# Attention scores of a transformer block on one core: six two-bank units per batch against four three-bank groups

## The chip, the core and the metric

The kernel runs on one core of a Trainium2 chip. The core's engines work in parallel, each on its own list of instructions in order, and wait for each other by semaphores: TensorE (PE in the profile, its weight loads PEld), VectorE (DVE), ScalarE (ACT), GpSimd (POOL) and SyncE (SP), which here issues the DMA transfers. The metric is the device time of one execution in microseconds (us). Matmul results go to PSUM, 8 banks of 512 float32 per partition.

## The reference

For 16 batches of 256 tokens with 256 features: a layer norm, then `x + attention(xn) + ffn(xn)`.

```
x + _L0_attn_ref(xn, w_qkv, w_out) + _L0_ffn_ref(xn, w_gating, w_linear)
attention, 16 heads of 16:  scores = where(causal, q k^T / 4, -1e10)
                            out = softmax(scores) v ;  out @ w_out
ffn, operands rounded to fp8: (gelu(x wg0) * (x wg1)) @ w_linear
```

## The kernel before

It has two phases. **The first** (lines 290 to 457 and 690 to 728) normalises the tokens in 8 chunks of 512, transposes them, and runs the feed-forward layer; the transposed tokens, split into a high and a low part (`xt_part`), are stored for the second phase (`xt_store`). The queries, keys and values of batch 0 and the queries and keys of batch 1 are already made inside it (`first_batches`).

**The second phase** is attention, one batch after another, software-pipelined by hand: the loops over `s` at the end of each engine's program name, stage by stage, which piece of which batch comes next. Nothing but this written order and the semaphores sets the sequence. A batch passes through these pieces:

- `project_qk` (L738) and `project_v` (L745): 12 matmuls each of 256 columns over all 128 rows of the array, into one of the two banks of `misc` (banks 6 and 7). `project_qk` is called twice a batch, for u = 0 and 1, eight heads each. ACT copies the result to `qk_raw` (`copy_qk`, L592), DVE rounds it to the high part (`round_qk`, L476), POOL subtracts for the low part (`split_qk`, L339), and SP issues three transfers that lay the parts out in `stack` (`fill_stack`, L228).
- The scores are computed twice. First for the row maxima (`max_scores`, L781): queries against keys, with the causal mask added by bf16 matmuls of a selection matrix (`pick`) and a triangle (`above`) (L773). DVE reduces each bank to the maxima (`find_max`, L494). `transpose_max` (L827) turns them, ACT negates them (`negate_max`, L606), and SP places them as one more row of `stack` (`place_max`, L233). Then again, transposed and with the maximum already subtracted by that row (`exp_scores`, L799); ACT takes the exponential into `arena` (`exponent`, L613) and POOL zeroes the part above the diagonal (`mask`, L352).
- `times_v` (L818): probabilities times values, 32 matmuls on four column tiles of the array, for c = 0 and 1. DVE transposes (`o_to_rows`, L501) and divides by the row sums (`normalize_o`, L507 to L516); ACT and POOL split the result (L622, L357), `project_out` (L835, 6 matmuls for each c) multiplies by the output weights, ACT copies (`copy_y`, L628), POOL adds the residual (L362), and SP stores.

All score matmuls use 63 or 64 rows of the array; those for u = 0 lie on the lower half of the rows and those for u = 1 on the upper, so that two run side by side. A batch has six **units** (`UNITS`), three for each half c of the heads: one unit of four heads with 128 keys, two of two heads with 256. A unit fills two banks. The maxima rotate over three banks (`max_ps`, banks 0 to 2), the exponentials have one pair (`exp_ps`, banks 3 and 4), and `times_v` has bank 5 (`pv_ps`). Unit n of batch s for the maxima and unit n of batch s-1 for the exponentials stand next to each other in the order; between such blocks stand the projections, the transposes and `times_v`. Stage `s` begins on PE with `exp_scores(s - 1, 0)`.

## Time and profile before

| | us |
|---|---|
| median of 3 runs | 386.46 |
| lowest and highest | 383.99, 386.74 |
| the profiled execution | 387.27 |
| its span in the trace | 385.5 |
| busy: PE, DVE, ACT, POOL | 357.1, 281.6, 222.9, 198.2 |

In the rows below a line starts with the time in us at which a group of instructions starts and the time it takes, then the engine, the source line, the operation, the tiles written and read, and the shape. Consecutive instructions of one line are merged ("x12"). Matmuls overlap in the records: what a block costs on PE is read from its start to the start of the next block, not from its duration.

### The profile page before, as it was taken

The numbers are of one execution on the slowest core, as the hardware profiler recorded it, in microseconds if no ns is written. First come the engines' busy times: TensorE is split into PE (matmuls) and PEld (weight loads), VectorE is DVE, ScalarE is ACT, GpSimd is POOL, SyncE is SP. The second block draws the span as 40 slices with busy tenths as digits, with TensorE's granted clock in tenths as the row PEclk, the third lists the DMA queues.
The fourth block names the chain that finished last, engine by engine and source line by source line (L and its number), as shares of the span: only waits on it lengthen the run. The fifth ranks groups of instructions, "written<-read, shape, count | busy, mean of one in ns | idle before, by whom it ended". The sixth has DMA issues, their size and how long they took to land.

```text
span 385.5 us, 9835 instructions
## 1 busy us (share of the span) xinstructions
PE 357.1 (93%) x3882; PEld 269.8 (70%) x3882; DVE 281.6 (73%) x540; ACT 222.9 (58%) x352; POOL 198.2 (51%) x236
## 2 busy tenths in 40 slices
PE   6698999998989799999999999999999999998884
PEld 6354455447474678788888888888888888885563
DVE  5778788876626657988778778878787887788832
ACT  0885666764645165656665656656666566574751
POOL 2352530333231234654847748568467485685575
PEclk9999999999999989999999999999999999998988
DMA  7986734940638114506347255274372562542002
GB/s 240 321 283 193 210 110 120 237 147 0 234 95 274 55 67 157 195 29 221 96 155 247 77 175 187 72 239 136 115 247 84 169 193 79 172 137 68 21 30 82
DMA packets 45453, 57.52 MB, mean 149 GB/s; under 512 B 2656, under 2 KB 36960, under 8 KB 45408
## 3 DMA queue, kind: packets, MB, share of 16 engines
q1 hardware_dynamic: 45408, 56.90, 45.8%
q8 instruction: 31, 0.51, 0.5%
q14 instruction: 14, 0.11, 0.1%
HBM read 16.78 MB, written 12.58 MB: 76 GB/s over the span
## 4 chain that ended last, share of the span: by engine, by line
PE 80%; DVE 8%; ACT 6%; issue 3%; DMA 1%; POOL 1%; POOLq 0%; DVEq 0%; SPq 0%; ACTq 0%
PE ps L738 12%; PE ps L818 12%; PE ps L799 11%; PE ps L781 8%; PE ps L726 7%; PE ps L745 7%; PE ps L835 6%; PE ps L773 4%; PE ps L706 4%; PE ps L699 4%; DVE act L457 4%; PE ps L827 2%; PE ps L675 2%; ACT arena L613 2%; ACT gate L562 2%
## 5 line engine op out<-in xcount | busy, mean ns | idle before, releaser
L494 DVE TENSOR_REDUCE row_max<-ps 128x2 f32<-128x512 f32 (+1 forms) x192 | 123.6, 686 | 43.9 <-PE ps L781 43.3
L613 ACT ACTIVATE arena<-ps 128x1024 f32<-128x1024 f32 x96 | 98.5, 1026 | 75.0 <-PE ps L799 75.0
L352 POOL TENSOR_SCALAR_AFFINE_SELECT arena<-arena 128x512 f32<-128x512 f32 (+1 forms) x96 | 73.7, 787 | 72.4 <-ACT arena L613 72.2
L799 PE MATMUL ps<-stack 64*128 64x256 f32 (+1 forms) x512 | 52.6, 305 | 4.1 <-ACT arena L613 4.1
L738 PE MATMUL ps<-xs,wq_part 128*128 128x256 f32 x384 | 53.7, 289 | 2.1 <-DVE wq_part L448 0.7
L457 DVE TENSOR_TENSOR act<-ps,gate 128x512 fp8e4<-128x512 f32 x64 | 43.1, 686 | 13.7 <-ACT gate L562 12.0
L781 PE MATMUL ps<-stack 63*128 63x256 f32 (+1 forms) x512 | 51.9, 301 | 0.0
L818 PE MATMUL ps<-arena,v_aug 128*32 128x256 f32 (+1 forms) x1024 | 50.6, 340 | 0.9 <-DVE xn L501 0.9
L738 PEld LDWEIGHTS ps<-xs,wq_part 128*128 128x128 f32 x384 | 48.7, 192 | 3.5 <-DVE wq_part L448 1.0
L799 PEld LDWEIGHTS ps<-stack 64*128 64x128 f32 x512 | 36.8, 190 | 18.1 <-issue 7.3
L562 ACT ACTIVATE gate<-ps 128x512 bf16<-128x512 f32 x64 | 38.0, 598 | 17.3 <-PE ps L699 11.1
L339 POOL TENSOR_TENSOR qk_part<-w_raw,qk_part 128x512 fp32r<-128x512 f32 x32 | 40.8, 1276 | 6.8 <-DVE qk_part L476 6.8
L706 PE MATMUL ps<-x,wg 128*128 128x512 fp8e4 x128 | 38.0, 378 | 4.9 <-DVE act L457 4.5
L818 PEld LDWEIGHTS ps<-arena,v_aug 128*32 128x32 f32 x1024 | 29.8, 113 | 17.3 <-issue 1.8
L699 PE MATMUL ps<-x,wg 128*128 128x512 fp8e4 x128 | 38.0, 379 | 2.1 <-ACT gate L562 1.0
L357 POOL TENSOR_TENSOR xt_part<-xn,xt_part 128x256 fp32r<-128x256 f32 x32 | 26.9, 841 | 23.8 <-ACT xt_part L622 23.7
L781 PEld LDWEIGHTS ps<-stack 63*128 63x128 f32 x512 | 36.4, 189 | 0.3
L773 PE MATMUL ps<-above,pick 64*128 64x128 bf16 (+1 forms) x384 | 31.0, 240 | 2.7 <-DVE row_max L494 2.7
L290 POOL TENSOR_SCALAR var_eps<-mean_var 128x4 f32<-128x4 f32 x8 | 2.1, 264 | 59.7 <-DVE mean_var L406 59.7
L835 PE MATMUL ps<-wq_part,xt_part 128*128 128x256 f32 x192 | 30.7, 296 | 0.8 <-ACT w_raw L628 0.7
L501 DVE STREAM_TRANSPOSE xn<-ps 128x512 f32<-128x512 f32 x32 | 22.8, 712 | 10.9 <-PE ps L818 10.9
L726 PE MATMUL ps<-wl,act 128*128 128x256 fp8e4 x256 | 29.4, 272 | 0.3 <-issue 0.3
(57 smaller groups left out, 440.7 us busy)
## 6 DMA issues: line engine op xcount, KB each, us to landing
stack<-qk_part SPq DMA_DIRECT2D x96, 256.0 KB, 3.0
xt_store<-xt_part SPq DMA_DIRECT2D x16, 512.0 KB, 4.1
xs<-xt_store SPq DMA_DIRECT2D x16, 512.0 KB, 4.3
out_dram<-w_raw SPq DMA_DIRECT2D x16, 256.0 KB, 4.3
xres<-in_L_attn_x_dram SPq DMA_DIRECT2D x7, 512.0 KB, 7.1
arena<-in_L_ffn_w_gating_dram SPq DMA_DIRECT2D x2, 1024.0 KB, 9.9
stack<-spare SPq DMA_DIRECT2D x4, 512.0 KB, 7.2
arena<-in_L_ffn_w_linear_dram SPq DMA_DIRECT2D x1, 1024.0 KB, 14.0
```

What stands on the lines that cost most here:

```text
L352: nc.gpsimd.affine_select(diag, diag, pattern=[[0, 1024 // width], [1, P]], compare_op=ALU.is_ge, fill=0.0, base=0, channel_multiplier=-1) ...
L457: nc.vector.tensor_tensor(act8[:, j, :], up_ps[j % 2][:], gate[:, j % 2, :], ALU.mult, saturate=False).then_inc(act_done, 1)
L494: nc.vector.tensor_reduce(row_max[:, b % 2, qt, col:col + heads], max_ps[:, place, :].rearrange("p (h k) -> p h k", k=width), axis=AXIS_X, ...
L613: nc.scalar.activation(arena[:, n, :, :], exp_ps, ACT.Exp).then_inc(exp_done, 1)
L699: last = nc.tensor.matmul(gate_ps[j % 2][:], wg8[:, 0, k, j * P:(j + 1) * P], x8[:, k, :], start=(k == 0), stop=(k == KD - 1))
L706: last = nc.tensor.matmul(up_ps[j % 2][:], wg8[:, 1, k, j * P:(j + 1) * P], x8[:, k, :], start=(k == 0), stop=(k == KD - 1))
L726: last = nc.tensor.matmul(down_ps[i][:, t * D:(t + 1) * D], act8[:, j, tok:tok + P], wl8[:, j, :], start=(j == 0), stop=(j == J - 1))
L738: last = nc.tensor.matmul(misc[:, 1, s * S:(s + 1) * S], wq_part[:, a, kt, col:col + P], xs[b % 2][:, z, kt, :], start=(i == 0), stop=(i = ...
L781: last = nc.tensor.matmul(max_ps[:, (2 * unit + u) % 3, i * width:(i + 1) * width], st[rows, j0 + i, 0, qt * P:(qt + 1) * P], st[rows, j0 ...
L799: last = nc.tensor.matmul(exp_ps[:, u, i * width:(i + 1) * width], st[rows, j0 + i, 1, kt * P:(kt + 1) * P], st[rows, j0 + i, 0, kt * P:S] ...
L818: last = nc.tensor.matmul(pv_ps[32 * i:32 * i + 32, u * S + kt * P:(u + 1) * S], va[:, kt, 2 * (HG * c + i) + u, :], cols, start=(kt == 0) ...
L835: last = nc.tensor.matmul(misc[:, 0, t * D:(t + 1) * D], ot_part[:, z, c, t * P:(t + 1) * P], wq_part[:, a, c, 3 * D:4 * D], start=(c == t ...
```

## The change

The scores of a batch come in four **groups** of three banks. Group (c, ii) fills the two first banks with one unit's two halves u, as before: for ii = 0 the four heads with 128 keys, for ii = 1 two heads with 256. Its third bank takes two heads with 256 keys of one half u = ii alone. The exponentials get banks 0 to 2 and the maxima banks 3 to 5; `times_v` moves to the two banks of `misc`, which it now shares with the projections, so that these are placed and waited for in another way (`pv_bank`, and the waits written out in the loop of PE).

On PE one function `scores(maxima, exps)` writes a block: all six mask matmuls of the group, the maxima of two banks, the exponentials of two banks (of another group), and then the third banks of both in turn, one matmul on one half of the rows and one on the other. The whole group waits, ahead of its masks, until DVE has reduced all three banks of the group before. DVE reduces two banks with one instruction of 1024 elements and the third with one of 512; ACT and POOL likewise have one instruction for two banks and one for the third. The rounding of queries and keys (`round_qk`) goes from DVE to ACT, which now reads the PSUM bank twice in `copy_qk`. `project_qk` writes one bank for u = 0 and the other for u = 1, both calls stand side by side in a stage, and so do `project_v` and both calls of `project_out`. The stages of all engines are written anew.

The banks, and the function that writes a block on PE:

```
-        max_ps, exp_ps, pv_ps, misc = ps[:, 0:3, :], ps[:, 3:5, :], ps[:, 5, :], ps[:, 6:8, :]
+        exp_ps, max_ps, misc = ps[:, 0:3, :], ps[:, 3:6, :], ps[:, 6:8, :]
...
+            def scores(maxima, exps):
+
+                if maxima:
+                    b, c, ii = maxima
+                    g = GROUPS * b + 2 * c + ii
+                    st = stack[b % NB]
+                    if g >= 1:
+                        pe.wait_ge(max_done, 2 * g)
+                    heads, width = (2, 2 * P) if ii else (4, P)
+                    for i in range(2):
+                        for u in range(2):
+                            put_mask(u, slice(64 * u, 64 * u + 64), heads, i)
+                        put_mask(2, slice(64 * ii, 64 * ii + 64), 2, i)
+                    if ii == 0:
+                        pe.wait_ge(stacked[c], 48 * (b + 1))
...
+                    if ei == 0:
+                        pe.wait_ge(neg_in[ec], 16 * (eb + 1))
+                    if h >= 1:
+                        pe.wait_ge(exp_done, 2 * h - 1)
...
+                if exps and h >= 1:
+                    pe.wait_ge(exp_done, 2 * h)
...
+                        last_max = nc.tensor.matmul(max_ps[:, 2, cols], st[rows, 4 * c + i, 0, P:S], st[rows, 4 * c + i, 1, :],
+                                                    start=False, stop=(i == 1), skip_group_check=True)
...
+                        last_exp = nc.tensor.matmul(exp_ps[:, 2, cols], est[rows, 4 * ec + i, 1, 0:P], est[rows, 4 * ec + i, 0, :],
+                                                    start=True, stop=True)
```

The copies of queries and keys on ACT:

```
             def copy_qk(b, g):
                 act.wait_ge(qk_ready[g], b + 1)
                 if b >= 1:
+                    act.wait_ge(stacked[g], 48 * b)
+                made = misc[:, g, :].rearrange("p (a s) -> p a s", a=2)
+                nc.scalar.copy(qk_part[:, g, QHI:KLO, :], made).then_inc(qk_hi[g], 1)
+                if b >= 1:
                     act.wait_ge(qk_lo[g], b)
-                nc.scalar.copy(qk_raw[:, g, :, :], misc[:, 1, :].rearrange("p (a s) -> p a s", a=2)).then_inc(qk_copied[g], 1)
+                nc.scalar.copy(qk_raw[:, g, :, :], made).then_inc(qk_copied[g], 1)
```

The new loop on PE, its calls and two of its waits:

```
+            for s in range(B + 3):
+                if has(s) or has(s - 2):
+                    scores((s, 0, 0) if has(s) else None, (s - 2, 1, 1) if has(s - 2) else None)
...
+                    project_qk(s + 1, 0)
...
+                    project_qk(s + 1, 1)
...
+                if has(s) or has(s - 1):
+                    scores((s, 0, 1) if has(s) else None, (s - 1, 0, 0) if has(s - 1) else None)
+                if has(s - 1) and s < B:
+
+                    pe.wait_ge(*((qk_copied[1], s + 2) if has(s + 1) else (o_by_q_done, turned(s - 2, 0))))
+                    transpose_max(s - 1, 1)
...
+                    times_v(s - 2, 1)
+                if has(s) or has(s - 1):
+                    scores((s, 1, 0) if has(s) else None, (s - 1, 0, 1) if has(s - 1) else None)
...
+                    project_v(s + 1)
...
+                    for c in range(2):
+                        project_out(s - 3, c)
...
+                if has(s) or has(s - 1):
+                    scores((s, 1, 1) if has(s) else None, (s - 1, 1, 0) if has(s - 1) else None)
...
+                    transpose_max(s, 0)
...
+                    times_v(s - 1, 0)
```

The loop on SP:

```
-            for s in range(B + 5):
-                if s >= 2 and has(s):
-                    fill_stack(s, 1)
-                if has(s - 1):
+            for s in range(B + 3):
+                if s == B:
                     place_max(s - 1, 1)
                 if s >= 1 and has(s + 1):
                     fill_stack(s + 1, 0)
+                    fill_stack(s + 1, 1)
+                if has(s - 1) and s < B:
+                    place_max(s - 1, 1)
```

On PE in a middle stage, before, from the masks of unit 0 to the exponentials of unit 1 (L773 masks, L781 maxima, L827 transposes of the maxima, L738 queries and keys, L799 exponentials):

```order
L773 MATMUL ps<-above,pick 128x4x64 [waits max_done]
L773 MATMUL ps<-above,pick 128x4x64 x3
L781 MATMUL ps<-stack 128x128 [waits stacked0]
L781 MATMUL ps<-stack 128x128 x7
L827 MATMUL ps<-ident,row_max 8x128 [waits max_done,v_done]
L827 MATMUL ps<-ident,row_max 8x128
L738 MATMUL ps<-xs,wq_part 128x256 [waits qk_copied0]
L738 MATMUL ps<-xs,wq_part 128x256 x11
L773 MATMUL ps<-above,pick 128x2x64 [waits max_done]
L773 MATMUL ps<-above,pick 128x2x64 x3
L781 MATMUL ps<-stack 128x256 x4
L799 MATMUL ps<-stack 128x256 [waits exp_done]
```

The same engine in the changed kernel, the first block of a stage (L771 masks, L793 maxima of two banks, L810 exponentials of two banks, L821 and L825 the third banks):

```order
L771 MATMUL ps<-above,pick 128x4x64 [waits max_done]
L771 MATMUL ps<-above,pick 128x4x64
L771 MATMUL ps<-above,pick 128x2x64
L771 MATMUL ps<-above,pick 128x4x64 x2
L771 MATMUL ps<-above,pick 128x2x64
L793 MATMUL ps<-stack 128x128 [waits stacked0]
L793 MATMUL ps<-stack 128x128 x7
L810 MATMUL ps<-stack 128x256 [waits exp_done]
L810 MATMUL ps<-stack 128x256 x3
L821 MATMUL ps<-stack 128x256 [waits exp_done]
L825 MATMUL ps<-stack 128x256
```

The masks of three banks stand ahead of the maxima, and the matmuls of one and a half units of each kind now stand in one block, between which and the next stand 24 matmuls over all rows or the transposes with `times_v`.

On SP, the transfers of one middle stage before (L233 negated maxima, L228 queries and keys, L218 tokens, L238 result):

```order
L228 DMA stack<-qk_part 32x4x512 [waits exp_ready,qk_lo1]
L228 DMA stack<-qk_part 32x8x256 x2
L233 DMA stack<-neg_max 2x4x256 [waits neg_done1]
L228 DMA stack<-qk_part 32x4x512 [waits exp_ready,qk_lo0]
L228 DMA stack<-qk_part 32x8x256 x2
L218 DMA xs<-xt_store 128x1024 [waits v_ready]
L238 DMA out_dram<-w_raw 128x2x256 [waits y_done]
L233 DMA stack<-neg_max 2x4x256 [waits neg_done0]
```

and in the changed kernel (L245 negated maxima, L240 queries and keys):

```order
L240 DMA stack<-qk_part 32x4x512 [waits exp_ready,qk_lo0]
L240 DMA stack<-qk_part 32x8x256 x2
L240 DMA stack<-qk_part 32x4x512 [waits exp_ready,qk_lo1]
L240 DMA stack<-qk_part 32x8x256 x2
L245 DMA stack<-neg_max 2x4x256 [waits neg_done1]
L230 DMA xs<-xt_store 128x1024 [waits v_ready]
L250 DMA out_dram<-w_raw 128x2x256 [waits y_done]
L245 DMA stack<-neg_max 2x4x256 [waits neg_done0]
```

The negated maxima of c = 1 now stand behind all six transfers of a batch's queries and keys.

## Rows read from the trace of the kernel before

**Rows 1.** The page: busy time of each engine, its share of the span, instructions.

```profile
PE 357.1 (93%) x3882; PEld 269.8 (70%) x3882; DVE 281.6 (73%) x540; ACT 222.9 (58%) x352; POOL 198.2 (51%) x236
```

**Rows 2.** Stretches (us): length, busy time of each engine, granted clock, DMA share, GB/s.

```profile
126.00:165.00 39.00, 35.64 (x439) 29.18 (x436) 28.26 (x48) 20.03 (x28) 16.11 (x18) 0.96 0.37 124
165.00:341.00 176.00, 176.00 (x2344) 147.23 (x2342) 140.23 (x254) 107.13 (x160) 113.33 (x124) 1.00 0.45 146
341.00:385.50 44.50, 34.33 (x440) 25.07 (x432) 26.14 (x48) 22.34 (x33) 28.20 (x33) 0.90 0.22 73
```

**Rows 3.** Timeline of PE, the first half of a middle stage.

```profile
226.45 0.66 PE L799 MATMUL ps<-stack 64*128 64x128 f32 x8
226.95 0.39 PE L773 MATMUL ps<-above,pick 64*128 64x256 bf16 x4
227.10 0.64 PE L781 MATMUL ps<-stack 63*128 63x128 f32 x8
227.67 0.38 PE L827 MATMUL ps<-ident,row_max 128*8 128x128 f32 x2
227.81 1.68 PE L738 MATMUL ps<-xs,wq_part 128*128 128x256 f32 x12
229.42 0.29 PE L773 MATMUL ps<-above,pick 64*128 64x128 bf16 x4
229.52 0.48 PE L781 MATMUL ps<-stack 63*128 63x256 f32 x4
229.84 0.40 PE L799 MATMUL ps<-stack 64*128 64x256 f32 x4
230.17 1.68 PE L745 MATMUL ps<-wq_part,xs 128*128 128x256 f32 x12
231.78 0.51 PE L799 MATMUL ps<-stack 64*128 64x256 f32 x4
...
232.63 1.51 PE L818 MATMUL ps<-arena,v_aug 128*32 128x256 f32 x32
234.06 0.66 PE L799 MATMUL ps<-stack 64*128 64x128 f32 x8
```

**Rows 4.** Timeline of PE: two adjoining blocks over all rows, and the next stage's start.

```profile
237.17 0.98 PE L835 MATMUL ps<-wq_part,xt_part 128*128 128x256 f32 x6
...
239.51 0.50 PE L799 MATMUL ps<-stack 64*128 64x256 f32 x4
...
241.81 0.66 PE L799 MATMUL ps<-stack 64*128 64x128 f32 x8
```

**Rows 5.** Timeline of PE: the first masks, and the starts of stages 3 and 15.

```profile
126.40 0.39 PE L773 MATMUL ps<-above,pick 64*128 64x256 bf16 x4
165.05 0.66 PE L799 MATMUL ps<-stack 64*128 64x128 f32 x8
347.81 0.55 PE L799 MATMUL ps<-stack 64*128 64x128 f32 x6
```

**Rows 6.** Timelines of DVE (two reductions) and of ACT (a copy, an exponential), middle stage.

```profile
230.04 1.29 DVE L494 TENSOR_REDUCE row_max<-ps 128x2 f32<-128x512 f32 x2 [0.97 <-PE ps L781]
226.09 0.61 ACT L592 COPY w_raw<-ps 128x512 f32<-128x512 f32 x1
227.15 1.02 ACT L613 ACTIVATE arena<-ps 128x1024 f32<-128x1024 f32 x1 [0.46 <-PE ps L799]
```

**Rows 7.** A stretch of the end, columns as in the second group.

```profile
352.80:356.00 3.20, 3.20 (x40) 0.53 0.00 0
```

**Rows 8.** The page: the subtraction for the low parts, mean ns and idle before.

```profile
L339 POOL TENSOR_TENSOR qk_part<-w_raw,qk_part 128x512 fp32r<-128x512 f32 x32 | 40.8, 1276 | 6.8 <-DVE qk_part L476 6.8
```

**Rows 9.** Waits from 341 us on: us in total, times, longest.

```profile
ACT arena L613 <- PE ps L799: 11.6, 12, 3.0
```

**Rows 10.** One line at a time: issue times in ns (min/median/max) and landing (us).

```profile
L228 SPq DMA_DIRECT2D stack<-qk_part x96: 542/606/1675, 97.8 to 346.4; - x96
DMA to landing us min/median/max: 2.4/3.0/5.7
```

More of the change, by code:

```diff
@@ L516, in normalize_o @@
                 nc.vector.transpose(ot_raw[:, c, :], o_norm[:, :]).then_inc(ot_ready, 1)
-            for s in range(B + 3):
-                if has(s - 1):
-                    find_max(s - 1, 5)
-                if s >= 1 and has(s + 1):
-                    round_qk(s + 1, 0)
+            for s in range(B + 2):
                 if has(s - 2):
@@ L752, in first_batches, with put_mask @@
                 pe.wait_ge(ffn_done, 2 * (CHUNKS - 2 + b))
-                project_qk(b, 0)
+                for g in range(2):
+                    project_qk(b, g)
                 if b == 0:
+                    pe.wait_ge(qk_copied[0], 1)
                     project_v(0)
-                pe.wait_ge(qk_copied[0], b + 1)
-                project_qk(b, 1)
             ffn_steps(step, first_batches)
-            def max_scores(b, n):
-                unit = UNITS * b + n
-                st = stack[b % NB]
-                heads, qt = (4, 0) if n % 3 == 0 else (2, 1)
+            def put_mask(bank, rows, heads, i):
@@ L784, in max_scores @@
[L784 to L802 removed]
+                first = width - P + 64 * i
@@ L840, in _ @@
             pe.wait_ge(act_done, J * CHUNKS)
+            pe.wait_ge(xt_lo, KD * CHUNKS)
             pe.wait_ge(spare_made, 1)
[L842 to L894 removed]
```

304 lines of the change are left out of this document (136 added, 168 removed).

## The prediction

> **What bounds the kernel.** I read the busy shares first: PE is busy 93% of the span, DVE 73% [rows 1]. A share says little by itself, so I cut the span into stretches [rows 2]. From 165 to 341 us PE is busy for 176.00 of 176.00 us at full granted clock; the list of waits for that stretch has none of PE's. DVE works 140 of the 176 us, ACT 107, POOL 113. So 45% of the run is a steady loop in which only PE's own time counts, and the rest is a first phase, the filling of the pipeline (35.6 of 39 us busy) and its emptying (34.3 of 44.5 us).
>
> In the loop the timeline of PE repeats every 241.81 - 226.45 = 15.36 us, one stage for one batch [rows 3, 4]. What counts is start to start. Two things are to be seen. Twelve matmuls over all rows take 1.61 us (L745, 230.17 to 231.78), but 18 in a row, from the second half of `project_out` to the end of `project_qk`, take 2.34 (237.17 to 239.51). So one more costs 0.12 us, and twelve of these are 1.48: about 0.15 us are paid for entering and leaving the block. Score blocks pay too: four masks, four maxima and four exponentials take 0.75 us where the masks come first (229.42) and 0.85 where the exponentials do (231.78). A stage has six score blocks, so six returns to the full array.
>
> **The change on PE in a steady stage.** The number of matmuls and their columns per batch are the same: masks 8 x 256 + 16 x 128 = 4096 columns before, and 2 x (4 x 256 + 2 x 128) + 2 x (6 x 128) = 4096 after. Removed are the switches. Block by block, from starts in [rows 3]:
>
> - A group with ii = 0: masks about 0.35 us (four 256-column masks take 0.15, 226.95 to 227.10, where both halves of the rows work side by side; the third bank's masks lie on one half and hold it up, 0.1 each); eight maxima 0.57 less the switch of 0.09, 0.48; four exponentials 0.24 (229.84 to 230.17 less 0.09); four matmuls of the third banks, on alternate halves, also 0.24; the switch 0.09. Sum 1.40.
> - A group with ii = 1: masks 0.22 (0.10 and 0.06 for each mask of the third bank), four maxima 0.32 (229.52 to 229.84), eight exponentials 0.44 (0.50 less the entry), third banks 0.24, switch 0.09. Sum 1.31.
> - 24 matmuls over all rows, twice: 1.61 + 12 x 0.12 = 3.05 each.
> - Transposes with `times_v` behind them, twice: 0.14 + 1.44 = 1.58 each.
>
> 2 x (1.40 + 1.31 + 3.05 + 1.58) = 14.68 us, against 15.36. For the masks the bounds are 0.1 us less a group (they overlap after all) and 0.1 more.
>
> The transposes used to be followed by full-array matmuls, now by `times_v` on 32-column tiles. No row shows that pair; the nearest are transposes into `project_qk`, contained in the 0.14, and scores into `times_v`, in the 0.09. The bounds are 0 and 0.15 a time; I take 0, as the transposes already pay on leaving the scores. The Trainium skill (TensorEngine Tiling (Array Packing), Key Properties) says that changing the tiling mode drains the engine. The 0.09 to 0.15 us at every change between blocks agree with it; by that rule the step from transposes to `times_v` is one more change of mode, and it would speak against this part of the edit.
>
> **What the others must deliver by then.** I lay one stage out from its first mask at 0. DVE starts 0.52 us after a block of four maxima starts (229.52, 230.04), that is 0.2 after the next block's start [rows 3, 6]; behind a switch, which holds the next block up by 0.1, I count 0.1.
>
> - DVE. Two reductions of 512 take 1.29 us, one 0.69 [rows 6], so one of 1024 is 1.2 to 1.3. In a ii = 1 group maxima are ready at 0.22 + 0.52 = 0.74; DVE is done with two banks at 2.0 and with the third at 2.65. The next group's masks come 1.31 + 1.58 = 2.89 after. That wait is covered by 0.2 us, the thinnest margin on DVE; behind ii = 0 the spacing is 4.45 and the margin large. DVE loses the two roundings and is busy some 12 of 14.7 us.
> - ACT. The second copies add 2 x 0.5 us; with exponentials 4 x (1.03 + 0.58) = 6.4 and the rest it is busy 11.4 of 14.7 us. The wait before the first transposes is for the second copy of u = 1: ready at 1.40 + 3.05 + 0.1 = 4.55, two copies of 0.6 overlapping by 0.1 [rows 6] end at 5.65, and the transposes stand at 4.45 + 1.31 = 5.76. Covered, by 0.1.
> - SP. The low parts are subtracted by POOL in 1.28 us [rows 8]: for u = 0 they are ready at 5.5, for u = 1 at 6.95. Six issues of 0.61 us with what lies between them [rows 10] run from 5.55 to 9.4; only then goes the transfer of the negated maxima of c = 1, which were ready at 7.4. The last group of the stage, at 1.40 + 3.05 + 1.31 + 1.58 + 1.40 + 3.05 = 11.8, needs them for its exponentials, 0.54 later at 12.3. The trace does not give its landing; the transfers ahead of it land after 2.4 us at best, 3.0 in the median, 5.7 at worst [rows 10]. That is 11.8, 12.4 or 15.1. I take 12.4, the median, since the six before it are just such transfers: a wait of 0.1. The Trainium skill (DMA: Bandwidth & Descriptors, Anatomy of one DMA) has a fixed cost of about 2.0 us for a transfer on GpSimd's path; if SP's were alike it would land at 11.4, and the wait would be nought.
>
> Period 14.68 + 0.1 = 14.8 us. PE goes through twelve stages between the third and the fifteenth: before 347.81 - 165.05 = 182.8 us (the last of them lacks half of its projection) [rows 5], after 12 x 14.8 = 177.6. **Gain 5.2 us.**
>
> **The ends.** The first phase: the second `project_qk` of batch 1 no longer waits for ACT's copy (0.95 us before); ACT's extra copies give half back, as its gelu comes behind them. Gain 0.4.
>
> Filling: before, from the first mask at 126.40 to stage 3, 38.65 us [rows 5]. In the new stage 0 nothing lies between the groups, so each waits for DVE: 2.9 + 2.6 + 2.9 + 2.6 = 11.0. Stage 1 meets the same waits and the wait for its exponentials, 13.1. Stage 2 is a steady one without `project_out`, 13.4. Before, PE fell once to half clock here; I leave one such stretch in, 1.2. Sum 38.7: no change, within 1.6 either way.
>
> Emptying: before, from 347.81 to the end 37.7 us. ACT waits there 12 times for exponentials' scores, 11.6 us in all [rows 9]; the last batch has four hand-overs of that kind instead of six, which gives some 2 us less; groups with no projections between them give 1.5 back in waits on DVE. Two stretches of half clock remain: the granted clock was 0.53 in the one [rows 7]. Gain 0.4, within 2.
>
> Sum: -5.2 - 0.4 - 0 - 0.4 = -6.0. The profiled execution took 387.27 us, of which 385.5 are the span; it becomes 381.3. It stood 0.8 above the median of the runs, so I put the median after at **380.5 us**.
>
> **Rivals.**
>
> - *The mode switch comes back.* `times_v` behind the transposes costs the upper bound, 0.15 us twice a stage: period 15.1, time 380.5 + 12 x 0.3 = 384. For it: every change of block seen in the trace costs that much. Against: the transposes have just paid it. This is the case that the rule on tiling modes would give. Chance 0.14.
> - *The wait for the whole group.* A group of masks now waits for all three banks; if DVE is later by 0.5 us than laid out (its reductions of 1024, or its division, which is held up beside POOL), 0.3 us are lost twice a stage: period 15.4, time 387.7, no change. For it: a margin of 0.2. Against: DVE has 2.7 us free a stage. Chance 0.17.
> - *The negated maxima stuck behind the six transfers.* Slower by over 1% means a median over 390.3, so a period over 15.6, so a wait over 0.9 us, so a landing over 3.8 us after the issue; between that and the worst row, at 4.5 to 5.0, the wait is 1.6 to 2.1 and the time about 400. For it: 5.7 us occurs. Against: the median is 3.0, and the load of tokens now comes behind. Chance 0.11.
> - *It saves more:* masks overlap, the filling is shorter: period 14.6, ends 2 better, 376. Chance 0.08.
>
> My own case keeps 0.50, with 377.5 to 383. Of it and the others: faster by over 1% (under 382.6; about what a measurement tells from none) 0.50 x 0.95 + 0.08 + 0.14 x 0.4 = 0.61; within 1% 0.27; slower 0.12. The range that leaves out the stuck transfers and half of the best case is 375.5 to 388.5.
>
> **What would show it.** In the timeline of PE a period near 14.8, with score blocks of 1.40 and 1.31, blocks of 3.05 over all rows, and `times_v` 0.14 behind the transposes. In the list of waits next to nothing of PE's between stages 3 and 15; a wait of masks on the reductions there means the second rival, one of the exponentials (L810) on the transfers the third. Reductions fall from 192 to 128 and DVE's busy time by some 18 us; ACT's rises by as much. In the filling waits of masks on DVE of about 1.5 us each. I would be wrong in the mechanism if the period fell without the switches getting fewer, or if half-clock stretches appeared inside the loop.

## The result, and the profile after

| | before | after |
|---|---|---|
| median of 4 runs each | 385.23 us | 390.34 us |
| lowest and highest | 383.68, 386.74 | 388.75, 391.20 |
| the profiled execution, its span | 387.27, 385.5 | 388.75, 386.7 |

The changed kernel takes 1.012 times as long (95% interval 1.0086 to 1.0154). The forecast was 380.5 us, with 375.5 to 388.5 as its range: the median lies outside it, and the sign is wrong. A second timing of the same kernel further below gave 1.0117.

The profiled execution of after is the fastest of its four; that of before, 387.27 us, is slower than all four timed ones. So the two traces differ by 1.5 us where the medians differ by 5. The traces say where the time goes; how much it is, the medians say.

The page of after, busy time, answers to [rows 1]:

```profile
PE 355.5 (92%) x3882; PEld 271.4 (70%) x3882; DVE 264.5 (68%) x444; ACT 238.8 (62%) x416; POOL 198.6 (51%) x268
```

DVE is busy 17.1 us less and ACT 15.9 more, as laid out. Next the stretches of after, columns as in [rows 2]: filling, steady stages, and then two pieces of the filling.

```profile
124.90:168.20 43.30, 37.10 (x417) 30.72 (x416) 25.75 (x32) 20.14 (x34) 14.57 (x19) 0.88 0.33 111
168.20:349.70 181.50, 181.13 (x2454) 152.42 (x2451) 134.59 (x192) 124.79 (x217) 120.84 (x157) 1.00 0.45 152
130.00:136.70 6.70, 6.31 (x40) 5.77 (x40) 2.29 (x4) 0.58 (x1) 0.00 (x0) 0.50 0.05 9
140.30:143.60 3.30, 3.30 (x18) 3.30 (x16) 0.97 (x2) 1.07 (x2) 0.25 (x1) 0.50 0.00 0
```

For a balance both kernels are cut at the same events, the first 256-column masks of each stage:

| us | before | after | change | forecast |
|---|---|---|---|---|
| start to the first mask | 126.40 | 124.91 | -1.5 | -0.4 |
| filling, to stage 3 | 39.15 | 43.30 | +4.2 | 0 |
| 12 steady stages | 182.75 | 181.48 | -1.3 | -5.2 |
| rest | 37.23 | 37.06 | -0.2 | -0.4 |

In the filling 10 us run at 0.50 of the full clock, which is the 1.2 GHz level, where before had one stretch of 3.4 us. And the steady stage gives 0.3 us at most where the forecast had 0.56. (Twelve times 0.3 would be more than 1.3: the last of before's twelve stages lacks half of its projection, which the forecast had allowed for, and after's have waits in them.) PE, a steady stage of after (L771 masks, L744 queries and keys, L853 transposes, L844 `times_v`, L751 values); it ends where the next begins, at 213.38:

```profile
198.33 0.39 PE L771 MATMUL ps<-above,pick 64*128 64x256 bf16 x4
...
199.74 3.13 PE L744 MATMUL ps<-xs,wq_part 128*128 128x256 f32 x24
202.80 0.29 PE L771 MATMUL ps<-above,pick 64*128 64x128 bf16 x4
...
204.11 0.38 PE L853 MATMUL ps<-ident,row_max 128*8 128x128 f32 x2
204.42 1.51 PE L844 MATMUL ps<-arena,v_aug 128*32 128x256 f32 x32
205.86 0.39 PE L771 MATMUL ps<-above,pick 64*128 64x256 bf16 x4
...
207.27 1.69 PE L751 MATMUL ps<-wq_part,xs 128*128 128x256 f32 x12
...
210.32 0.28 PE L771 MATMUL ps<-above,pick 64*128 64x128 bf16 x4
...
213.38 0.34 PE L771 MATMUL ps<-above,pick 64*128 64x256 bf16 x3
```

From start to start: group with ii = 0 1.41, 24 matmuls 3.06, group with ii = 1 1.31, and 24 matmuls 3.05. These four are the forecast's 1.40, 3.05, 1.31, 3.05. Transposes with `times_v` take 0.31 + 1.44 = 1.75 where it had 1.58. The period is 15.05 us against 15.36 [rows 3, 4] and the 14.8 of the forecast.

Stage 0 of after on PE, its four groups with the values ahead of the last, then the next stage's first masks:

```profile
124.91 0.39 PE L771 MATMUL ps<-above,pick 64*128 64x256 bf16 x4
...
127.79 0.29 PE L771 MATMUL ps<-above,pick 64*128 64x128 bf16 x4 [1.64 <-DVE row_max L500]
...
130.39 0.61 PE L771 MATMUL ps<-above,pick 64*128 64x256 bf16 x4 [1.68 <-DVE row_max L500]
...
132.53 2.93 PE L751 MATMUL ps<-wq_part,xs 128*128 128x256 f32 x12
135.38 0.40 PE L771 MATMUL ps<-above,pick 64*128 64x128 bf16 x4
...
138.45 0.39 PE L771 MATMUL ps<-above,pick 64*128 64x256 bf16 x4 [1.21 <-DVE row_max L500]
```

The second and third group and the next stage wait until DVE has reduced all three banks (L500 is the reduction of the third); ahead of the fourth stand the values. After the first idle spells the granted clock halves: `project_v` takes 2.85 us from start to start, against 1.61 in [rows 3]. Before had waits in these places too, of 0.8, 0.8 and 0.5 us, and its single stretch at half clock came later, at 134.0. Last, PE's list of waits over the whole of after:

```profile
PE ps L771 <- DVE row_max L500: 6.8, 5, 1.7
...
PE ps L810 <- DMA stack<-neg_max: 1.1, 2, 0.7
```

The second line is the third rival in a small form: the exponentials wait for the negated maxima. One of the two waits, of 0.74 us, is in the filling, one in the loop. A third doesn't show as a wait of PE: in the stage that starts at 213.38, exponentials start 0.61 us after the matmul ahead of them, whose neighbours lie 0.1 apart. Two stages of the loop take 15.64 and 15.34 us for it.

Three causes are thus on the table. **A**: transposes directly ahead of `times_v` cost 0.175 us a time more than the forecast had, 4.2 us in 12 stages. **B**: the wait for the whole group costs time in the filling, by PE's idleness and by the clock that falls after it. **C**: the negated maxima come too late behind six transfers. Of B there are two readings: the waits themselves, or only the clock.

### The profile page after: what moved, and what is told of

Same layout as the page of the kernel before. It is cut to its first block, busy times and chain, and to the rows that moved or that the text cites. A ratio compares the mean times of both kernels' runs of the same rounds, so it can differ in the third digit from the quotient of the medians.

```text
span 386.7 us, 9837 instructions
## 1 busy us (share of the span) xinstructions
PE 355.5 (92%) x3882; PEld 271.4 (70%) x3882; DVE 264.5 (68%) x444; ACT 238.8 (62%) x416; POOL 198.6 (51%) x268
## 4 chain that ended last, share of the span: by engine, by line
PE 77%; DVE 9%; ACT 3%; issue 3%; POOL 3%; DMA 2%; SPq 1%; POOLq 0%; DVEq 0%; ACTq 0%
PE ps L744 13%; PE ps L844 11%; PE ps L732 7%; PE ps L751 6%; PE ps L793 6%; PE ps L861 5%; PE ps L810 5%; PE ps L771 5%; PE ps L712 4%; PE ps L705 4%; DVE act L472 4%; PE ps L821 3%; PE ps L825 2%; PE ps L853 2%; PE ps L681 2%
## 5 line engine op out<-in xcount | busy, mean ns | idle before, releaser
L497 DVE TENSOR_REDUCE row_max<-ps 128x8 f32<-128x1024 f32 x64 | 78.2, 1223 | 46.9 <-PE ps L793 42.8
L619 ACT ACTIVATE arena<-ps 128x1024 f32<-128x1024 f32 x64 | 65.6, 1025 | 46.1 <-PE ps L810 44.8
L368 POOL TENSOR_SCALAR_AFFINE_SELECT arena<-arena 128x1024 f32<-128x1024 f32 x64 | 55.3, 864 | 41.4 <-ACT arena L619 41.4
L744 PE MATMUL ps<-xs,wq_part 128*128 128x256 f32 x384 | 51.6, 291 | 1.4 <-DVE wq_part L463 0.7
L744 PEld LDWEIGHTS ps<-xs,wq_part 128*128 128x128 f32 x384 | 48.3, 194 | 3.8 <-DVE wq_part L463 1.0
L844 PE MATMUL ps<-arena,v_aug 128*32 128x256 f32 (+1 forms) x1024 | 49.1, 333 | 0.7 <-POOL arena L372 0.7
L562 ACT ACTIVATE gate<-ps 128x512 bf16<-128x512 f32 x64 | 37.9, 598 | 17.1 <-PE ps L705 11.0
L793 PE MATMUL ps<-stack 63*128 63x128 f32 (+1 forms) x384 | 45.6, 297 | 0.0
L500 DVE TENSOR_REDUCE row_max<-ps 128x2 f32<-128x512 f32 x64 | 43.5, 680 | 0.3 <-PE ps L821 0.2
L844 PEld LDWEIGHTS ps<-arena,v_aug 128*32 128x32 f32 x1024 | 29.4, 111 | 18.6 <-issue 7.8
L810 PE MATMUL ps<-stack 64*128 64x128 f32 (+1 forms) x384 | 40.9, 281 | 1.5 <-DMA stack<-neg_max 1.1
L621 ACT ACTIVATE arena<-ps 128x512 f32<-128x512 f32 x64 | 37.9, 592 | 0.0
L810 PEld LDWEIGHTS ps<-stack 64*128 64x128 f32 x384 | 34.0, 188 | 3.7 <-DMA stack<-neg_max 2.6
L793 PEld LDWEIGHTS ps<-stack 63*128 63x128 f32 x384 | 36.0, 192 | 0.0
L771 PE MATMUL ps<-above,pick 64*128 64x128 bf16 (+1 forms) x384 | 29.3, 240 | 6.8 <-DVE row_max L500 6.8
L382 POOL TENSOR_TENSOR w_raw<-w_raw,xres 128x512 f32<-128x512 f32 x16 | 20.4, 1272 | 26.0 <-ACT w_raw L636 26.0
```

Of the source, the lines that this page charges most:

```text
L368: nc.gpsimd.affine_select(diag, diag, pattern=[[0, 1024 // width], [1, P]], compare_op=ALU.is_ge, fill=0.0, base=0, channel_multiplier=-1) ...
L497: nc.vector.tensor_reduce(to[:, :, 4 - heads:4], max_ps[:, 0:2, :].rearrange("p e (h k) -> p e h k", k=width), axis=AXIS_X, op=ALU.max).th ...
L500: nc.vector.tensor_reduce(row_max[:, b % 2, 1, PAIRS * c + 4 * ii:PAIRS * c + 4 * ii + 2], max_ps[:, 2, :].rearrange("p (h k) -> p h k", k ...
L619: nc.scalar.activation(arena[:, 3 * c + 2 * ii, :, :], exp_ps[:, 0:2, :], ACT.Exp).then_inc(exp_done, 1)
L744: last = nc.tensor.matmul(misc[:, u, s * S:(s + 1) * S], wq_part[:, a, kt, col:col + P], xs[b % 2][:, z, kt, :], start=(i == 0), stop=(i = ...
L771: nc.tensor.matmul(max_ps[:, bank, :].rearrange("p (h k) -> p h k", k=width)[:, :, first:first + 64], pick[rows, i, :], above[rows, :].uns ...
```

## The experiments

| kernel | median, runs | against before | filling | 12 stages | rest |
|---|---|---|---|---|---|
| after, again | 389.87, 4 | 1.0117 (1.0049 to 1.0185) | 42.95 | 181.64 | 36.42 |
| transposes moved | 387.90, 10 | 1.0014 (0.9982 to 1.0045) | 41.87 | 179.20 | 40.10 |
| filling kept busy | 389.29, 10 | 1.0083 (1.0049 to 1.0116) | 41.41 | 182.21 | 37.11 |
| split wait | 385.17, 10 | 0.9984 (0.9952 to 1.0017) | 37.83 | 184.58 | 35.59 |
| maxima between | 388.14, 10 | 1.0055 (1.0029 to 1.0081) | 43.66 | 180.56 | 37.97 |
| split, maxima between | 382.19, 9 | 0.9903 (0.9869 to 0.9936) | 38.23 | 181.42 | 35.03 |
| moved, busy, split | 380.07, 4 | 0.9827 (0.9788 to 0.9866) | 39.13 | 176.56 | 38.51 |
| moved, split | 380.11, 4 | 0.9821 (0.9781 to 0.9860) | 39.49 | 176.56 | 37.77 |
| moved, split, end | 378.21, 4 | 0.9758 (0.9703 to 0.9814) | 37.98 | 176.56 | 36.20 |
| rounding on DVE | 398.92, 6 | 1.0337 (1.0305 to 1.0368) | 43.47 | 191.01 | 36.42 |

The last three columns (us) are from the one profiled execution of each, cut as in the table above. The runs come from three chips. Before itself had a median of 386.71 us beside "transposes moved", "filling kept busy", "split wait" and "moved, busy, split", of 385.86 beside "split, maxima between" and "rounding on DVE", and of 385.83 beside the others. So kernels from different chips are better compared by their ratios to before than by their medians; a ratio is uncertain by 0.3 to 0.7%.

**The change once more**, without an edit, beside the second set of experiments.

> The changed kernel once more, on the same chip as the next three, so that they can be set against it. All theories: 1.0 to 1.3% above the kernel before; steady period 15.04 us, filling 43 us, mean granted clock of a run 0.975 to 0.981.

389.87 us, ratio 1.0117. The slowdown is real, and the trace has the same parts: half clock for 6.8 and 3.4 us in the filling, stages of 15.05.

**A: the transposes moved** ahead of blocks over all rows, where they stood before the change; ACT's negations and SP's transfers follow them. With that the transfer of the negated maxima of c = 1 stands ahead of the six again, so this edit undoes C as well as A.

```
                     scores((s, 0, 0) if has(s) else None, (s - 2, 1, 1) if has(s - 2) else None)
+                if has(s - 1):
+                    pe.wait_ge(*((o_by_q_done, turned(s - 2, 0)) if s >= 2 else (v_done, 2)))
+                    transpose_max(s - 1, 1)
                 if s >= 1 and has(s + 1):
                     project_qk(s + 1, 0)
...
                     scores((s, 1, 0) if has(s) else None, (s - 1, 0, 1) if has(s - 1) else None)
+                if has(s):
+                    transpose_max(s, 0)
                 if has(s + 1):
                     project_v(s + 1)
```

> The changed kernel with both pairs of transposes of the maxima moved away from the place ahead of times_v: those of c = 1 ahead of project_qk, those of c = 0 ahead of project_v, so that they border on matmuls over the whole array; negations and their transfers move with them. Theory A (a change between transposes and the four column tiles of times_v is a switch of its own, 0.17 us each): the steady period falls from 15.04 to 14.69 us, and the two or three waits for negated maxima inside the loop (1.1 us in all) go, since that transfer now stands ahead of the six of queries and keys; some 5 us less in all, about 385. Rival B (times_v costs the same wherever the transposes stand, and what is missing lies in the filling alone): period 15.0, time within 1.5 us of the changed kernel.

Measured 387.90 us. The ratio is 1.1% under after's, some 4 us. PE in a steady stage of it (L849 transposes, L740 queries and keys, L840 `times_v`):

```profile
198.26 0.38 PE L849 MATMUL ps<-ident,row_max 128*8 128x128 f32 x2
198.40 3.24 PE L740 MATMUL ps<-xs,wq_part 128*128 128x256 f32 x24
201.58 0.29 PE L767 MATMUL ps<-above,pick 64*128 64x128 bf16 x4
...
202.88 1.51 PE L840 MATMUL ps<-arena,v_aug 128*32 128x256 f32 x32
204.32 0.39 PE L767 MATMUL ps<-above,pick 64*128 64x256 bf16 x4
```

The transposes cost 0.14 us again, and `times_v` still 1.44. So the same two instructions cost 0.31 ahead of 32-column tiles and 0.14 ahead of the full array: A is shown, 0.17 us a time. But each block of 24 has grown from 3.06 to 3.18, so the period falls only by 0.11 us, to 14.93, where 14.69 was expected. Inside the block two starts lie 154 and 224 ns apart where the others, behind the first, lie 114 to 126: it is the place where the second `project_qk` waits for ACT to have negated the maxima out of its bank. The other block has the same two spacings (150 and 224 ns) where `project_out` waits for the other negation. The waits for the negated maxima on the DMA are gone in this trace. The rest takes 3 us more than in after. There `project_out` of the last stage with scores stands behind the transposes and waits 1.3 us for their negation on ACT, and this execution had 10.7 us at half clock in its rest, against 4.2 in after's.

**B: PE kept busy in the filling**, by 44 more transposes that nobody reads, in stage 0 alone.

```
+            def stay_warm(n):
+                for i in range(n):
+                    nc.tensor.transpose(exp_ps[:, 0, 0:P], ident[:], ident[:])
...
+                if s == 0:
+                    stay_warm(16)
```

> The changed kernel with 16, 16 and 12 extra transposes of the identity into an unused bank behind the first, second and fourth score block of stage 0, where PE waits for VectorE. Theory A (the filling is long because PE falls to half clock in its waits for whole groups: 10.2 us of half clock there against 3.4 before): no or one stretch of half clock, the filling from the first mask to stage 3 falls from 43.3 to about 39.5 us, time 3 to 4 us less. Rival B (the filling is bounded by the waits on VectorE and ScalarE themselves, at whatever clock): under 1 us less.

Measured 389.29 us; the ratio is 0.4% under after's, which is within the uncertainty. Stage 0 on PE:

```profile
126.15 1.97 PE L834 MATMUL ps<-ident 128*128 128x128 f32 x16
...
131.97 1.68 PE L751 MATMUL ps<-wq_part,xs 128*128 128x256 f32 x12
133.68 0.29 PE L771 MATMUL ps<-above,pick 64*128 64x128 bf16 x4
...
136.28 0.39 PE L771 MATMUL ps<-above,pick 64*128 64x256 bf16 x4
```

The granted clock stays full (1.00 from 124.9 to 136.3), `project_v` takes 1.7 us, and stage 0 ends after 11.29 us and not 13.54. That is the clock's share, 2.2 us. But the run as a whole hardly gains. In its profiled execution the exponentials wait longer for the negated maxima right behind (rows of the wait list, 124 to 346 us):

```profile
PE ps L810 <- DMA stack<-neg_max: 3.3, 3, 1.9
PE ps L771 <- DVE row_max L500: 0.9, 1, 0.9
```

Its stage 2 takes 15.73 us, where a kernel without these waits takes 13.6. So the clock alone isn't what the change lost, and C takes the place of what B gives up.

**B: the wait split.** The third bank's masks stand behind the two-bank matmuls, and only they wait for DVE's second reduction.

```
                     if g >= 1:
-                        pe.wait_ge(max_done, 2 * g)
+                        pe.wait_ge(max_done, 2 * g - 1)
...
-                        put_mask(2, slice(64 * ii, 64 * ii + 64), 2, i)
...
+                if maxima:
+                    if g >= 1:
+                        pe.wait_ge(max_done, 2 * g)
+                    for i in range(2):
+                        put_mask(2, slice(64 * ii, 64 * ii + 64), 2, i)
```

> The changed kernel with one part of the change undone: a group's masks of the two first banks wait only for the reduction of these two banks of the group before, and the masks of the third bank stand behind the exponentials, with the wait for its reduction. Theory A (the whole-group wait costs 0.6 us at every group in stages 0 and 1 and nothing in the loop): intervals of groups in stage 0 fall from 2.9 to 2.2 us, filling 3 us shorter with the half clock it brings; in the loop the period rises by 0.1 to 0.3 us, as four more times a batch bf16 masks stand between float32 matmuls; net 0 to 3 us less. Rival B (the masks at the front are what saves in the loop): period up by 0.4 us or more, time not lower.

Measured 385.17 us: the ratio is 1.4% under after's, some 5 us, and level with before. Stage 0 on PE, where L497 is the reduction of two banks:

```profile
124.90 0.39 PE L771 MATMUL ps<-above,pick 64*128 64x256 bf16 x4
...
127.01 0.28 PE L771 MATMUL ps<-above,pick 64*128 64x128 bf16 x4 [0.91 <-DVE row_max L497]
...
128.91 0.39 PE L771 MATMUL ps<-above,pick 64*128 64x256 bf16 x4 [0.73 <-DVE row_max L497]
...
133.55 0.39 PE L771 MATMUL ps<-above,pick 64*128 64x256 bf16 x4 [0.59 <-DVE row_max L497]
```

The waits are half as long, the stage takes 8.65 us instead of 13.54, and the filling 37.8 instead of 43.3, at full clock in this execution. Three kernels with split waits below had 6.8 us of half clock in stage 0, as after had, and took 11.2 to 11.4 us for it. So of the 4.9 us between 13.54 and 8.65 the wait itself is 2.1 to 2.4 and the clock 2.5 to 2.8; the kernel kept busy says the same from the other side, 11.29 us at full clock with the whole group waited for. The filling as a whole is no guide here: in this one the negated maxima take back some 2 us (stages 1 and 2 take 14.47 and 14.72 us, and 13.37 and 13.68 where the same kernel has C undone, below). Splitting the wait does not keep the clock up by itself, then. Over the ten executions the mean granted clock was 0.986 to 0.992, against 0.975 to 0.981 in after's first four, but one trace of a split kernel below has as much half clock in its filling as after. In the loop every block is 0.015 to 0.02 us longer, 0.07 a stage, and C grows (the list of waits, 124 to 350 us):

```profile
PE ps L809 <- DMA stack<-neg_max: 3.4, 6, 1.0
```

**C: the negated maxima between** the two sets of queries and keys on SP.

```
                     fill_stack(s + 1, 0)
-                    fill_stack(s + 1, 1)
                 if has(s - 1) and s < B:
                     place_max(s - 1, 1)
+                if s >= 1 and has(s + 1):
+                    fill_stack(s + 1, 1)
```

> The changed kernel with one thing in the transfer queue's order: the transfer of the negated maxima of c = 1 stands between the transfers of queries and keys of u = 0 and those of u = 1, instead of behind all six. Theory C (that transfer, queued behind six of 256 KB, lands too late in some stages: waits of 1.0 us in stage 2 and 1.1 in the loop of the profiled execution of the changed kernel, 3 us and more in others): no wait of PE for it, filling 1 us shorter, twelve stages in 180.5 us instead of 181.5 to 182.2, time 1.5 to 3 us less. Rival (it comes late for another reason, the negation on ScalarE or the load on the DMA engines): the waits stay, time within 0.5 us.

Measured 388.14 us, 0.6% under after. SP's queue in after and then in this kernel, one stage each (they start at 244.06 and 244.21):

```profile
249.74 3.95 SPq L240 DMA_DIRECT2D stack<-qk_part  x6
253.73 0.56 SPq L245 DMA_DIRECT2D stack<-neg_max  x1
```

```profile
249.88 1.88 SPq L240 DMA_DIRECT2D stack<-qk_part  x3
251.80 0.56 SPq L245 DMA_DIRECT2D stack<-neg_max  x1
```

The transfer goes out 2.1 us earlier, no wait for it is left in the trace, and every stage takes 15.05 us: 180.56 for twelve, 0.9 less than in after's trace. Stage 2 takes 13.62 us, where after took 14.60. C is shown in the traces. In the times it is worth some 2 us: 1.7 by the medians, both from one chip, and 0.6% by the ratios. It is clearer on top of the split wait, next. The execution had 17.1 us of half clock in its filling, more than any other here; so its filling is no measure.

**B and C undone together**, with the transposes where the change put them. It asks whether the causes add up.

> Changed kernel with two edits: the third bank's masks stand behind the two-bank matmuls and wait for DVE's second reduction there, and the transfer of the negated maxima of c = 1 is issued between the two sets of queries and keys. The transposes stay where the change put them, directly ahead of times_v. If the three losses add (the wait for the whole group, the negated maxima, transposes into times_v), the filling is about 38 us as with the split wait alone (37.83), the twelve stages lose the waits for the negated maxima, which cost 3 us there (184.58 against 12 x 15.12 = 181.4), and come to 181.4, and the time is some 382 us, 0.8 per cent under before. Rival: the filling's gain came from that run's undisturbed clock alone; then it is over 41 us again and the time 385 to 386, no different from before. Second rival: the negated maxima were late because of ACT, not because of their place; then waits of 0.5 us and more of the exponentials on them remain and the stages stay at 183 to 185.

Measured 382.19 us, 382 expected. The filling is 38.2, the stages 15.12, the list of waits of PE from 165 to 345 us is empty. Against the split wait alone C gives 0.8%, and 3.2 us in the twelve stages. B and C are worth 2.2% together, some 8 us, and with A still in it the kernel beats before by 1.0%.

**A and B undone together**, with the extra transposes of the filling and then without. As moving the transposes undoes C too, nothing of the three is left here.

> All three edits together. If the three losses (mode switch, half clock, whole-group wait) are separate, their gains add: period about 14.8 us, filling about 37 us, time about 378 to 380, below both kernels. If the half clock in the filling is only a consequence of the whole-group wait, the extra transposes add nothing and may cost up to 1 us.

> Moved transposes and split wait, without the extra transposes in the filling. In the kernel with all three edits these ended later than VectorE was ready. If half clock in the filling follows from the whole-group wait: filling 37.5 us or less against 39.1, time 1 to 2 us under 380. If it is a trouble of its own: stretches of half clock come back in stages 0 and 1, filling 40 us, time about 381. Steady period 14.71 either way.

380.07 and 380.11 us: the extra transposes give nothing once the wait is split. With them stage 0 took 11.11 us at full clock, where the split wait alone had taken 8.65: they end later than DVE is ready. Without them it took 11.41, with 6.8 us of half clock. The second kernel's filling came out as 39.5 and not 37.5: half clock came back in stages 0 and 1, 6.8 and 3.4 us, as in after. So the second reading held: it is not merely a consequence of the wait for the whole group.

Both have stages of 14.71 us, 0.41 less than the 15.12 of the kernel above with B and C undone. That is A once more, 4.9 us in twelve stages. In the traces the edits do more together than apart. Alone, moving the transposes shortened the stage by 0.11 us and splitting the wait lengthened it by 0.07; together they shorten it by 0.34. In the times (ratios 1.1%, 1.4% and 3.0% under after's) the excess is no larger than the uncertainty. On PE it is seen at a stage's start up to its second group (here with the end mended, below):

```profile
192.58 0.39 PE L771 MATMUL ps<-above,pick 64*128 64x256 bf16 x4
...
194.00 0.38 PE L857 MATMUL ps<-ident,row_max 128*8 128x128 f32 x2
194.14 3.11 PE L744 MATMUL ps<-xs,wq_part 128*128 128x256 f32 x24
197.18 0.28 PE L771 MATMUL ps<-above,pick 64*128 64x128 bf16 x4
```

The 24 matmuls take 3.04 us again. The reason stands on ACT: first the transposes-moved kernel (its stage starts at 196.86), then this one (192.58), the exponential and the negation:

```profile
198.14 1.02 ACT L617 ACTIVATE arena<-ps 128x1024 f32<-128x1024 f32 x1 [1.10 <-PE ps L806]
...
199.54 0.36 ACT L608 ACTIVATE neg_max<-ps 8x256 fp32r<-8x256 f32 x1
```

```profile
193.70 1.03 ACT L619 ACTIVATE arena<-ps 128x1024 f32<-128x1024 f32 x1 [1.06 <-PE ps L809]
...
195.09 0.36 ACT L610 ACTIVATE neg_max<-ps 8x256 fp32r<-8x256 f32 x1
```

The exponential starts 1.28 us after the first mask with all masks in front, and 1.12 with the third bank's behind. The negation is over 0.17 us sooner, and PE does not stop in the middle of its block.

**The end mended**: in the last stage the transposes stay where the change had them.

```
-                if has(s):
+                if has(s) and s < B - 1:
                     transpose_max(s, 0)
```

> The same, with the last stage of the maxima (s = 15) in the order of the changed kernel: project_out ahead of the transposes of c = 0, and these behind the last score block, as there is no project_v there to hide their negation. Measured with the transposes moved: a wait of 1.1 us of project_out for the negation and one of 0.5 of masks on VectorE, and an end of 38.5 to 40.1 us against 35.6 to 37.1. Expected: an end of 36 to 37 us, time 1.5 to 2.5 us less than without it. Rival (the longer end is half clock that would fall elsewhere too): same time within 0.5 us.

378.21 us, the fastest kernel here: 0.976 of before (0.970 to 0.981) and 3.6% under after by the ratios. In its twelve stages PE is busy for all of 176.60 us, where before took 182.75; the stretch, columns as above:

```profile
163.10:339.70 176.60, 176.60 (x2454) 153.11 (x2448) 134.04 (x192) 124.39 (x217) 121.18 (x157) 1.00 0.47 157
```

The mending itself was worth 1.9 us of the medians. The two intervals overlap, but the rest fell from 37.8 to 36.2 us in the traces, with about as much half clock in both (4.7 and 4.4 us).

**The rounding back on DVE**, all else as in after.

```
-                nc.scalar.copy(qk_part[:, g, QHI:KLO, :], made).then_inc(qk_hi[g], 1)
...
+                nc.vector.tensor_copy(qk_part[:, g, QHI:KLO, :], qk_raw[:, g, :, :]).then_inc(qk_hi[g], 1)
```

> Changed kernel with one edit: the rounding of queries and keys is on DVE again, as before the change, and ACT reads the PSUM bank once. This tests whether moving it mattered. Theory: little. The period stays 15.04 to 15.05, set by PE; in the filling DVE is what PE waits for, and two roundings of 0.7 us a batch more on it lengthen stage 1 and 2 by up to 1.4 us each where they stand ahead of a reduction, 43.3 to 44 or 45; ACT's copies of 0.6 us fall away in the first phase, 0.3 us gained. Time 389.5 to 392. Rival: the second copies on ACT delayed the exponentials and the negation, and so the negated maxima; then the waits of the exponentials on them vanish, the twelve stages fall from 181.5 to 180.6, and the time is under that of the changed kernel by 1 us or more.

398.92 us; the ratio is 2.2% over after's, some 8 us. I had expected next to nothing, and neither of the two readings holds. DVE in one stage (L490 rounding, L524 division, L506 and L509 reductions), and PE's masks behind it:

```profile
235.38 0.43 DVE L490 CAST qk_part<-w_raw 128x512 fp32r<-128x512 f32 x1 [0.94 <-ACT w_raw L606]
...
236.00 1.45 DVE L524 TENSOR_TENSOR o_norm<-xn,r_den 128x256 f32<-128x256 f32 x1
...
237.86 0.39 DVE L490 CAST qk_part<-w_raw 128x512 fp32r<-128x512 f32 x1
238.16 1.22 DVE L506 TENSOR_REDUCE row_max<-ps 128x4 f32<-128x1024 f32 x1
239.29 0.68 DVE L509 TENSOR_REDUCE row_max<-ps 128x2 f32<-128x512 f32 x1
```

```profile
240.03 0.39 PE L781 MATMUL ps<-above,pick 64*128 64x256 bf16 x4 [0.81 <-DVE row_max L509]
```

The first rounding waits 0.94 us for ACT's copy, and what stands behind it on DVE waits with it. The division then falls into the time of POOL's subtraction, and takes 1.45 us; at this place of after it falls into the time of one of POOL's masks, and takes 0.64. Here is POOL's subtraction, and then the division and POOL's mask in after:

```profile
235.89 1.28 POOL L352 TENSOR_TENSOR qk_part<-w_raw,qk_part 128x512 fp32r<-128x512 f32 x1 [0.89 <-DVE qk_part L490]
```

```profile
201.34 0.64 DVE L515 TENSOR_TENSOR o_norm<-xn,r_den 128x256 f32<-128x256 f32 x1
```

```profile
201.30 0.41 POOL L372 TENSOR_SCALAR_AFFINE_SELECT arena<-arena 128x256 f32<-128x256 f32 x1
```

The division starts 0.11 us after the subtraction and ends 0.28 after its end; in after it starts 0.04 after the mask and ends 0.27 after that one's end. The same holds in all twelve traces of this case. In 338 of their 384 divisions an instruction of POOL had more than 0.2 us still to run when the division started, and the division ended 0.27 to 0.29 us after that one's end, whether it was long or short; the 46 others took 0.42 to 0.43 us. The Trainium skill (SBUF — State Buffer, SBUF: two separate sides) has a pair of ports that DVE, in an operation with two inputs from SBUF, and GpSimd can only hold in turn, whoever starts first; the rows agree with it. Then comes the second rounding, so the reductions end late, and the masks of the whole group wait 0.81 us, once in every stage: period 15.92. That is the forecast's second rival. It did not happen in the loop of after, where the rounding had gone to ACT: there the last reduction of a ii = 1 group ends at 205.35 and the next masks start at 205.86, a margin of 0.5 us where I had laid out 0.2, part of it A's longer transposes.

## Why the prediction was wrong

The mechanism on PE was right in its main part. The six blocks became four, and their sizes, 1.40, 1.31 and twice 3.05, came out to about 0.01 us. In the score blocks that is the sum of their terms; in the trace maxima, exponentials and third banks interleave, and the terms can't be read one by one. Taken by the profiled executions the forecast said 379.5 for the span and 386.7 came. Of these 7.2 us:

1. **"Transposes with `times_v` behind them: 0.14 + 1.44"** is the step that failed in the loop. I took the low bound, 0, "as the transposes already pay on leaving the scores"; measured are 0.175 us a time, a little over the high bound of 0.15: 12 x 0.35 = 4.2 us. The rival that named it gave 384. The starts of single instructions show how it is paid. After the second transpose the first matmul of `times_v` starts 203 ns later, and a full-array matmul 28 ns later. From scores to the transposes it is 200 to 207 ns too, and from scores to `times_v` 206 to 210. So the transposes behave like the full-array matmuls: they had paid for the change away from the scores, and `times_v` pays for another. This agrees with the Trainium skill (TensorEngine Tiling (Array Packing), Key Properties), by which a change of the tiling mode drains the engine; the transposes use 8 columns of the array and `times_v` tiles of 32. I had the sentence and set it aside for a reason that is true, and that only covers the first of the two changes.
2. **"Sum 38.7: no change"** failed in the filling: 43.3. The first waits of the groups were forecast as they came (2.88 and 2.60 us from group to group, 2.9 and 2.6 laid out). Between the third and the fourth stand the values, which the forecast had not laid out; at full clock the wait covers them (2.88 us from group to group in the kernel kept busy, 4.99 in after). The three stages took 13.54, 15.16 and 14.60 us where 11.0, 13.1 and 13.4 were laid out, with 1.2 for half clock besides. What I left out is what follows PE's idleness: I kept one stretch of half clock, because before had one, though each wait was twice as long. It became 10.2 us. In stage 0 that costs 2.2 us, as the kernel kept busy shows (11.29, near the 11.0). The stretch of 3.4 in stage 1 costs 1.5: two kernels that are alike there, with it and without, took 14.81 and 13.31. In stage 2 it is the negated maxima, 1.0 us. It is an error of method too: I judged the wait for the whole group by the steady stage, where it is covered, and it is in the filling, without work between the groups, that it costs most. Split, it gives some 5 us.
3. **"A wait of 0.1"** for the negated maxima, every stage: in the trace 0 in most stages and 0.3 to 1.0 in a few, 0.9 in the loop in all, which is about the 1.2 that 12 x 0.1 makes. That the sum comes near is luck, since no stage had the wait as I described it. The times of after with and without it differ by some 2 us, and where it falls in the filling (0.74 in one wait) I had not counted it.
4. **The first phase** gained 1.5 and not 0.4 us. 0.7 of it was already there at 88 us, ahead of the projections, and is chance of the execution: in the second trace of after it is 0.2. Behind that point both traces gain 0.75. Of these 0.9 come at the second `project_qk` of batch 1 and 0.5 are given back before the first masks, which is the 0.4 of the forecast; the other 0.3 lie ahead of that projection and are not explained.
5. **The emptying** was right, 0.2 gained for 0.4.

The two other causes of the distance between 380.5 and 390.3 lie in the choice of executions: 0.8 us of before's profiled run over its median, 1.6 of after's below.

Of the rivals the first happened in full, the third in small, and the second in the filling only. Each had been given a price as if it came alone. Their prices were 3.6, 7 and far more, so two of them together were enough for "slower", and I had given that 0.12. What speaks against adding is also in the runs: the transposes moved alone give 0.11 us a stage of their 0.35, because the negation that then stands in front of the second `project_qk` is late by the masks.

Left open: why the negated maxima are late in one stage and not in the next with the same issue time in the stage; how the half-clock stretches of the filling come out, from none to 17.1 us over these executions; and how much fewer they are with the wait split.

## What to carry to other kernels

Count every change of tile shape in the new order, also between two small blocks that had never been neighbours, and price an unseen pair at the dearest change that the trace shows. Lay a coarser wait out in the filling as well as in the steady stage: there little covers it, and the clock can fall after it. When a producer writes several banks for one consumer, wait for each bank where it is first written, not for all at the front.

## What the runs showed of the hardware that was not expected

- Two 128-column transposes with 8 columns of weights cost 0.138 us ahead of a full-array matmul and 0.313 ahead of matmuls on 32-column tiles.
- A short wait inside a run of 24 full-array matmuls shows as spacings of 154 and 224 ns instead of about 119 each, so 0.14 us, at a place where the list of waits shows nothing.
- Masks of a third bank, which lie on one half of the rows, ahead of the matmuls of both halves delay ACT's first exponential of the block by 0.16 us, though the block as a whole is as long (1.41 and 1.42 us).
- One DVE reduction of 1024 elements takes 1.22 us, two of 512 took 1.29 [rows 6]; one ACT exponential of 512 takes 0.59.
- A DVE division of 256 elements with both inputs in SBUF takes 0.43 us. Started while an instruction of POOL on SBUF runs, it ends 0.27 to 0.29 us after that one's end: 0.64 us in most stages of after, 1.45 beside a subtraction.
